# A graph layer on one core: the main path's branch put directly behind the load of the flag

## The reference, cut to what matters

```python
xw = jnp.einsum('nd,rdh->nrh', x, W_rel)            # 16 relations
messages = xw[src, edge_type]
agg = jax.ops.segment_sum(messages, dst, num_segments=NUM_NODES)
out = relu(agg + x @ W_self + bias)
...
xn = _layernorm(x)
x = x + gnn(xn, src, dst, edge_type, ...) + mix(xn[None], ...)[0]
x = x + ffn(_layernorm(x)[None], ...)[0]
```

## Time and profile before

| | us |
|---|---|
| median of 3 runs | 2344.6 |
| lowest and highest | 2341.38, 2349.25 |
| the profiled execution: its own time | 2342.61 |
| its span in the profile | 2341.0 |
| PE, POOL, DVE, ACT busy in the span | 1988.8, 1713.7, 1268.4, 683.9 |

### The profile page before, as it was taken

How to read it: one execution, slowest core, us unless ns; L and a number is a source line. 1 busy time by engine, 2 the same in 40 slices (tenths; PEclk the granted TensorE clock), 3 DMA queues, 4 the chain that set the end, 5 groups by cost and what they waited for, 6 DMA issues and landing times.

```text
span 2341.0 us, 53372 instructions
## 1 busy us (share of the span) xinstructions
PE 1988.8 (85%) x18206; PEld 1629.0 (70%) x18206; DVE 1268.4 (54%) x4442; ACT 683.9 (29%) x1713; POOL 1713.7 (73%) x1789
## 2 busy tenths in 40 slices
PE   0268878879888889998898898899999898898897
PEld 0256657657666667777787787787777787787786
DVE  6766545654564555465465465455454555545543
ACT  1322222222232232333233233233233333332332
POOL 3477777777777777777777777777777777777771
PEclk9979999999999999999999999999998999999998
DMA  7555444444444444444444444444444444444441
GB/s 214 190 155 146 138 129 137 143 131 130 145 140 128 138 143 125 136 125 122 126 136 121 126 136 121 127 137 122 125 136 121 127 131 126 126 129 128 126 128 37
DMA packets 158303, 310.49 MB, mean 133 GB/s; under 512 B 37682, under 2 KB 100635, under 8 KB 157774
## 3 DMA queue, kind: packets, MB, share of 16 engines
q0 software_dynamic: 82832, 228.83, 34.4%
q1 hardware_dynamic: 73725, 78.47, 10.3%
q10 hardware_dynamic: 1508, 0.02, 0.0%
HBM read 275.24 MB, written 31.96 MB: 131 GB/s over the span
## 4 chain that ended last, share of the span: by engine, by line
PE 58%; POOL 15%; issue 9%; DVE 8%; DMA 6%; ACT 2%; DVEq 0%; POOLq 0%; ACTq 0%; SPq 0%
PE bank L1365 15%; POOL ring L537 15%; PE bank L1384 14%; PE bank L1387 7%; DMA ring<-table,idx_now 4%; PE bank L1379 4%; PE bank L1501 3%; PE bank L1480 2%; DVE hot L1011 2%; PE bank L1407 2%; PE bank L1496 1%; PE bank L1526 1%; DVE s_lo L1030 1%; PE bank L1523 1%; PE bank L1524 1%
## 5 line engine op out<-in xcount | busy, mean ns | idle before, releaser
L537 POOL DMA_INDIRECT ring<-table,idx_now x1715 | 1667.0, 972 | 515.9 <-issue 483.3
L1365 PE MATMUL bank<-hot,ring 128*128 128x256 f16 (+10 forms) x9408 | 784.7, 237 | 184.4 <-DMA ring<-table,idx_now 84.3
L1365 PEld LDWEIGHTS bank<-hot,ring 128*128 128x128 f16 x9408 | 675.7, 99 | 261.6 <-DVE hot L1011 96.6
L1011 DVE TENSOR_SCALAR hot<-iota,key_now,hot_v 128x272 f16<-128x272 f16 (+8 forms) x1723 | 514.2, 350 | 20.8 <-PE bank L1365 1.7
L1384 PE MATMUL bank<-wr,s_hi 128*128 128x256 f16 x3136 | 370.7, 278 | 0.0
L1384 PEld LDWEIGHTS bank<-wr,s_hi 128*128 128x128 f16 x3136 | 314.6, 100 | 59.3 <-issue 13.1
L685 ACT ACTIVATE s_hi<-bank 128x512 f16<-128x512 f32 x392 | 212.0, 593 | 283.1 <-PE bank L1365 280.7
L1030 DVE SCALAR_TENSOR_TENSOR s_lo<-s_hi,bank 128x512 f16<-128x512 f16 x392 | 250.4, 679 | 30.1 <-ACT s_hi L685 28.2
L1039 DVE SCALAR_TENSOR_TENSOR u_g<-bank,x_g 128x256 f32<-128x256 f32 x49 | 20.6, 421 | 315.4 <-PE bank L1387 315.4
L1387 PE MATMUL bank<-wr,s_lo 128*128 128x256 f16 x1568 | 187.2, 273 | 0.0
L1387 PEld LDWEIGHTS bank<-wr,s_lo 128*128 128x128 f16 x1568 | 153.4, 98 | 17.8
(11 more groups left out here) (228 smaller groups left out, 2021.3 us busy)
## 6 DMA issues: line engine op xcount, KB each, us to landing
ring<-table,idx_now POOLq DMA_INDIRECT x1715
work<-table SPq DMA_DIRECT2D x49, 128.0 KB
xnt_d<-work SPq DMA_DIRECT2D x49, 128.0 KB
xnt_g<-xnt_d SPq DMA_DIRECT2D x49, 128.0 KB
q2nt_d<-work SPq DMA_DIRECT2D x49, 128.0 KB
work<-q2nt_d SPq DMA_DIRECT2D x49, 128.0 KB
x_g<-x SPq DMA_DIRECT2D x48, 128.0 KB
u_d<-u_g SPq DMA_DIRECT2D x48, 128.0 KB
```

The costliest lines, as they stand in the source:

```text
L537: pool.indirect_dma_start(ring[:, b, :], None, own, bass.IndirectOffsetOnAxis(ap=idx_now[:, parity, b:b + 1], axis=0), oob_is_err=False)\
L1011: dve.tensor_scalar(hot[:, b % OH, 0:w], iota16[:, lo * R:hi * R], key_now[:, b:b + 1], hot_v[:, b % BLOCKS:b % BLOCKS + 1], ALU.is_equal, ...
L1365: last = mm(banks[2 * (q % 2) + h][:, (l - q * BANK_N) * R:(r - q * BANK_N) * R], ring[:, b, part * D + h * P:part * D + (h + 1) * P], hot ...
```

## The change

The branch with `gather_all(table)` is moved from behind the general path to directly behind the load of the flag. Nothing else is changed: the same instructions stand in every engine's program, and only POOL's are in another order.

```diff
             pool.wait_ge(s["flag_ready"], 1)
             general = pool.value_load(flag[0:1, 0:1])
+            with pool.If(general < 1):
+                gather_all(table)
             with pool.If(general > 0):
 
                 for k, (full, own) in enumerate(((dst_p, dst), (src_p, src), (typ_p, etype))):
...
                 gather_all(sums_t)
-            with pool.If(general < 1):
-                gather_all(table)
```

## The result

The changed kernel took 2333.61 us in the median of 11 runs (2329.79 to 2337.22), and the kernel before, run beside it, 2340.93 us (11 runs, 2333.3 to 2349.25). The ratio is 0.9968, with a 95% interval of 0.9955 to 0.998, that is 7.5 us faster, 4.7 to 10.5. A second measurement gave 0.9965 (0.9952 to 0.9979). I had forecast 2338.9 us from a gain of 5.7 us.

What follows compares the result with a forecast made beforehand. POOL's gathers, waiting for nobody from first to last, were taken to set the pace. Removing the 5.62 us gap and L609's 0.04 us gave 2344.6 - 5.7 = 2338.9 us, range 2334.0 to 2345.0.

Steps and rivals of the forecast that it cites:

- the far pass: POOL's branch L551 over the general path, ahead of the first gather: 5.62 us, read as waiting for code behind weight loads.
- the tail: From the last gather's end to the kernel's end: its landing and fixed work up to 2336.15 + 0.42 us.
- Removed: Ahead of the first gather: the 5.62 us pass from L551 and L609's 0.04 us go, together 5.66 us.
- First gather: POOL's first gather starts at 102.43 - 5.66 = 96.77 us.
- Early gathers beside DVE: About four gathers in the gained time might lose 0.62 us each to DVE's splits, 2.5 us in all; taken as zero.
- PE's block 18: In the first tile, PE's 5.21 us wait for DVE stays, so PE leaves no earlier, maybe a microsecond later.
- Moved behind: At the end, L553 passes over the general path; a 5.62 us gap there is covered and costs nothing.
- Last gather: POOL's last gather ends near 2290.4 us, in place of 2296.07.
- A: Ahead of the first gather: the gap has another cause and only changes its name; time stays 2344.6 us; chance 0.05.
- B: At the start: early gathers held beside weight loads and DVE; gain 0 to 3 us, 2341.6 to 2344.6; chance 0.06.
- C: POOL's moved gather loop fetched anew at each of 24 returns: 43 us slower, 2388 us; chance 0.02.
- D: PE has no room to follow the earlier gathers; time 2343 to 2344.6 us; chance 0.04.

Runs made afterwards that it cites:

- near: Kernel before, its unexecuted general path without gather_all(sums_t), so the branch passes over 53 instructions in place of 206; ratio 0.9979, again 0.9977.
- mid: Kernel before, the general path's gather_all(sums_t) cut to the first tile without loop, so the branch passes over 90 instructions; ratio 0.9974.
- place208: Kernel before, the general path's gather_all(sums_t) replaced by three first tiles without loop, branch over 164 instructions; gap 5.68 us, one execution 2333.95 us.
- twice: Kernel before, with gather_all(sums_t) called twice in the unexecuted general path, branch over 359 instructions; ratio 0.9995.
- quiet: Kernel before, with SP's weight loads held until POOL's first index copy; gap 2.80 us, ratio 0.9985.
- hoist: Changed kernel, with the first index copy and the flag's load moved ahead of POOL's wait for the table stores; ratio to before 0.9967.
- delay: Changed kernel, with 30 fills on POOL (11.07 us) between the branch and the first index copy; ratio to before 1.0017.
- match: Changed kernel, with 16 fills on POOL between the branch and the first index copy, to start gathers where the kernel before does; ratio to before 1.0.

## Why the prediction was wrong, and where it was right

**The mechanism was right.** POOL set the pace, never waited, and the gap behind L551 was a fetch of code that the far pass had made necessary. It went down to 0.10 us, and nothing took its place. `near`, `mid`, `place208` and `twice` show a step that fits held or not held and no cost by distance, `quiet` that POOL waits for the fetch and that it queues on the DMA engines, and the ten timed rows that the first gather's start reaches the end, one for one within their scatter.

**The step that failed** is the last of the sum: "That execution stands 2.0 us under the median of the runs, so the median comes to 2344.6 - 5.7 us". The median of three runs was no level. The same three runs are among the eleven that the result was taken beside, and the other eight have a median of 2340.2 us. In all the comparisons the kernel before had medians of 2338.19 to 2340.93 us, with single runs from 2333.24 to 2349.25, and my 2344.6 was 3.7 us over the one beside the result. On the level of 2340.93 the same gain gives 2335.3 us, against 2333.61 measured. The remaining 1.7 us are the term of the gain: 5.7 forecast, 7.5 (4.7 to 10.5) measured, and 6.0 from the first gather's start. The step of 2.0 us had even its sign wrong. I put the median 2.0 us over the profiled execution. It lies 1.7 us under it in the kernel before (2340.93 against 2342.61) and 3.1 us under it in the changed kernel (2333.61 against 2336.71); in `hoist`, `delay`, `match` and the second timing of `near` the profiled execution was the slowest of all.

On the profiled execution's own scale the forecast held: span 2335.3 us forecast, 2335.1 measured. That it came within 0.2 us is luck. I had called the tail fixed and left the stretch as it was; the one came out 3.0 us longer and the other 3.0 us shorter, and they cancelled.

**The range** gave the scatter 4.9 us below the centre, and with the centre 3.7 us too high its lower end came to 2334.0 us. The same 4.9 us below 2335.3 would have reached down to 2330.4.

**The steps one by one.** *Removed*: 5.66 us forecast, 5.66 found. *First gather*: 96.77 forecast, 96.44 found. *Early gathers beside DVE*: I took zero of 0 to 2.5 us, and they ran at 0.95 to 1.01 us. Later gathers met DVE's splits in their place, and the 41st starts 6.4 us earlier than before. *PE's block 18*: expected no earlier, it came 1.2 us earlier, and with its wait of 4.74 us for DVE it still had nothing to do with the gathers. *Moved behind*: L553 ran at 2272.4 us and the next instruction of POOL's sequencer, the drain, at 2274.9, some 2.5 us later and 55 us before the last DVE instruction. The pass over the general path costs there about what it cost in `quiet` (2.49 to 2.80 us), beside DMA engines that were 54% busy, and nobody waits. *Last gather*: 2290.4 forecast, 2287.11 found, and the tail gave the difference back.

**The rivals.** *A* (the gap is not the far pass) is out by the chain of the changed kernel and by the four other places of the target. With it goes the reading by which the target lay within what is held. The Trainium skill, page "Runtime: NRT & Kernel Launch", section "Instruction fetch mechanics", has blocks of 256 instructions and two of them held, which would put places 208 and 250 inside, and 403 too unless some hundred instructions stand ahead of the program. The stall that it describes for a target outside is what the runs show, but the reach is shorter here: held at 134 and not at 208, in packets of 8 KB (88 of them, 0.72 MB, in either kernel). *B* (eaten at the start) is out by the early gathers' durations. *C* (the loop at its new place) is out, since from 250 to 837 us queue 14 moved nothing in the changed kernel either, its packets are the same 88 in the whole execution, and the changed kernel is faster and not 43 us slower. *D* (PE cannot follow, a gain of 0 to 1.6 us) is out by the result, whose interval begins at 4.7 us, and by `near`, `mid` and `hoist`; `delay` adds that there is no slack for a later start either.

## What to carry to other kernels

A branch over code that does not run is not free where the engine behind it sets the pace. Put the path that runs right behind the branch, and look for a gap of "issue" between two branch rows of an engine's sequencer. Where DMA transfers are queued at that moment, the same fetch cost twice as much here. A packet of an instruction queue inside such a gap is a hint and no proof: `near` and `mid` moved one as well. And a gain of 0.3% in a kernel whose runs scatter by that much is better read from the one gap and the first instruction behind it than from medians of three.

## What the runs showed of the hardware that I had not expected

- POOL's fetch has a step, not a slope: 0.45 us to a target 53 or 90 instructions on, 5.6 to 5.7 us to one 164, 206 or 359 on, all at the same moment of the program. The two near ones move an instruction packet too, and do not wait for it.
- The same fetch took 2.5 to 2.8 us with idle DMA engines and 5.6 us behind weight loads that filled them to 107%, although it is a single packet of 0.3 to 0.4 us. The packet starts 1.24 us behind the branch in the one case and 3.84 us in the other.
- POOL's sequencer leaves the loop 15 us ahead of the last gather, with twelve gathers issued and not yet run. That a fetch inside the loop would be covered by this lead is argued and was not tried.
- The executions of one kernel lie up to 16 us apart (7.4 us in the changed one, 16.0 in the one before, each in 11 runs). In the profiles the same 1715 gathers are busy between 1659.9 and 1671.2 us in all, and the tail behind them is 37.6 to 43.7 us long.
